# One-core transformer layer (feed-forward, attention, feed-forward): the order of the small steps inside an attention slot, the lag of the first slot, and the entry of the second feed-forward phase

## Chip, cores and metric

One core of a Trainium2 chip. The metric is the time of one execution on the device in microseconds. Lower is better.

## The reference

x has 16 sequences of 256 tokens of 128 channels. The layer is a gated feed-forward block, an attention block, and the same feed-forward block again, each on a layer norm of x and added to x:

```python
x = x + 0.5 * ffn(layernorm(x))      # silu(x W1 s1) * (x W2 s2), two hidden layers of 512 with exact gelu, then W3
x = x + attn(layernorm(x))           # 16 heads of 8 channels: softmax(q k^T / sqrt(8)) v, then Wo + bo
x = x + 0.5 * ffn(layernorm(x))
```

All of it is fp32. The kernel keeps that accuracy with pairs of high and low parts (`act_hi`/`act_lo`, `x_hi`/`x_lo`) for PE's fp32r matmuls.

## The kernel before

The whole x lies in SBUF. There are three phases: `ffn_phase(0)`, attention, `ffn_phase(1)`. Each engine has its own hand-written program, ordered against the others by semaphores only, so the order in which the code calls things is the order in which the engine does them.

**Attention.** A batch is one sequence (256 tokens), 16 batches in 8 pairs. The function `attend(b, ...)` of every engine does one *slot*: slot b computes, in 16 steps u = 0 to 15,

- the row maxima of batch b + 1: PE `max_scores` (L1179, two matmuls a step into one of three rotating banks), DVE `max_unit` (L883, one reduce a step). PE may write a bank again only when DVE has reduced what stood in it, three steps earlier;
- the scores of batch b for the softmax: PE `scores` (L1191 and L1193, four matmuls), ACT `exp_unit` (L678, one exp of 128x512 a step). They run SKEW = 4 steps behind, so units 12 to 15 fall into steps 0 to 3 of the next slot (`in_step`);
- PE `weigh` (L1204): after every fourth unit of scores, sixteen matmuls of probabilities with V, 1.0 us in all. It falls at steps 3, 7, 11 and 15;
- small steps that all use PSUM bank 6 in turn: `max_rows` (u = 1) with ACT `top_max` and DVE `split_max`, which makes `m_parts` for the scores; `transpose_o` and `project_out` of batch b - 2 (u = 3, 5) with ACT `o_to_sbuf` between them and DVE `add_att` (L912, u = 6) behind; `tokens_of_o` of batch b - 1 (L1222), which needs `evacuate_o` (ACT, u = 7), and behind it DVE `norm_o` (L900) and `scale_o` (L904);
- for a pair of batches that comes later, still on bank 6: in odd slots (argument `ahead`) `transpose_att` at u = 7 (L1156), `project_q` at u = 9 (L1161), `project_k` at u = 11 (L1165); in even slots (argument `v_pair`) `project_v` at u = 9 (L1169). ACT copies each out of bank 6 (L571 for q and k). DVE has the layer norm of that pair spread over its steps (`norm_steps`, `normalise`, dictionaries `odd` and `even`).

A **pair of steps** below means an even step and the odd one behind it: their matmuls go to different rows of the array and run together.

q and k then go to DRAM and back, to be laid out by head: ACT `high_part`, POOL `low_part` (L471), SyncE `write_qk` (eight DMAs of 256 KB, L353), and, when all eight have landed, two `load_qk` of 1 MB (L361), the first of which slot 2i + 3 needs at its first step for q and k made in slot 2i + 1. `tokens_of_o` comes at TOKENS = 13, so `norm_o` and `scale_o` come at 14 and 15, and `max_rows` of the next slot waits for `scale_o` (semaphore `o_norm`).

**Behind the last slot.** `attend(NBATCH, own=False)` does the eight steps that are left of batch 15: the last scores, then `transpose_o` and `project_out` of batch 14, and the last weighing at u = 7. `layer1` of the second phase follows: eight tiles, each a gate and an up matmul group (L1092), ACT's silu (L544) and high part (L536), DVE's product (L842) and low part (L833). Between its tiles sit the last small steps for batch 15. ACT loads the gelu table (L518) when the last high part is done (`body`, `first`).

The lines that must be seen exactly:

```python
if u == TOKENS and own and prev:
    if ahead is not None:
        pe.wait_ge(k_full, ahead)
    elif v_pair is not None:
        pe.wait_ge(v_set, v_pair + 1)
    elif prev2:
        pe.wait_ge(att_added, b - 1)
    tokens_of_o(b - 1)
```

Of the kernel before, what the change touches and what calls it, by code (L numbers as in the profile page):

```python
# [27 lines left out]
ACT = mybir.ActivationFunctionType  # L28
# [23 lines left out]
TOKENS = 13  # L52
# [14 lines left out]
def macaron_kernel(nc, x, w_ffn, w_att, s12, sg, s3, bqk, bv, bo, eye, sel, low_rows, out):  # L67
# [11 lines left out]
    with ctx:  # L79
# [210 lines left out]
        def in_step(u, prev, own=True):  # L290
# [105 lines left out]
        def _(pool):  # L396
# [62 lines left out]
            def max_again(b, bb):  # L459

                for qt in range(2):
                    pool.wait_ge(max_done, UNITS * b + 8 * qt + 8)
# [3 lines left out]
                        .then_inc(max_twice, 1)  # L466

# [22 lines left out]
            low_parts(2)  # L490
            pool.wait_ge(bias_set, 1)
            with pool.Fori(1, NPAIR - 2) as i:
                max_again(2 * i, 0)
# [4 lines left out]
                low_parts(i + 2)  # L498
            max_again(NBATCH - 4, 0)
# [13 lines left out]
        def _(act):  # L513
# [24 lines left out]
            def layer1(n0, between={}):  # L538


                for t in range(L1_TILES):
# [55 lines left out]
            def ffn_phase(f):  # L597
                t1, t2, nb = f * NB * HT, f * NP * HID_TILES, f * NB

                def body(i, first=False, more=True):  # L600
# [6 lines left out]
                    if first:  # L607
                        last_product()
                        load_table(ACT.Gelu)
# [55 lines left out]
                else:  # L665
                    layer1(t1, {0: lambda: evacuate_o(NBATCH - 1), 3: lambda: o_to_sbuf(NBATCH - 1)})
# [27 lines left out]
            def attend(b, bb, prev=True, prev2=True, own=True, steps=UNITS, ahead=None, v_pair=None):  # L694


                for u in range(steps):
                    for d, v in in_step(u, prev, own):
                        if v < UNITS:
                            exp_unit(b - d, (bb + d) % 2, v)  # L700
                        if v == UNITS + 3 and own:
                            evacuate_o(b - d)
                    if u == (1 if prev else 0) and own:
                        top_max(b, 6 if prev else 4)
                    if u == 3 and prev2:
                        o_to_sbuf(b - 2)
                    if u == (9 if prev else 5) and v_pair is not None:
# [3 lines left out]
                    if u in (9, 11) and ahead is not None:  # L711
                        full_part(ahead, (u - 9) // 2)
                    if u in (10, 12) and ahead is not None:
                        high_part(ahead, (u - 10) // 2)
# [4 lines left out]
            def att_body(i, par, ahead=True, more=True, first=False):  # L719
                attend(2 * i, 0, prev=not first, prev2=not first, v_pair=(i + 1, 1 - par) if more else None)  # L720
# [779 lines left out]
```

## Time and profile before

| | |
|---|---|
| median of 3 runs | 623.62 us (618.94 to 626.49) |
| the profiled execution, own time | 617.05 us |
| span in its profile | 615.2 us |
| busy: PE, PEld, ACT, DVE, POOL | 589.1, 439.3, 466.4, 443.6, 98.3 us |

The span runs from the first to the last instruction; the profiled execution took 1.9 us more than that. All starts below are in us from the span's start. "PE" is TensorE's matmuls and "PEld" its weight loads, which overlap them; their durations overlap each other too, so the distance from one start to the next says more than a duration. The chain that ended last is followed back from the last instruction, at each step to what released it. A bracket behind an instruction gives the idle time of its engine before it and who ended it. Phase 1 takes about 0 to 204 us, the attention slots 204 to 436, the second feed-forward phase the rest.

### The profile page before, as it was taken

What the parts mean: (1) busy time and instruction counts of PE and PEld (TensorE: products, weight loads), DVE (VectorE), ACT (ScalarE), POOL (GpSimd) and SP (SyncE); (2) the same over time, 40 slices, a digit from 0 to 9 for tenths busy, and PEclk for the clock granted to TensorE, in tenths of its full rate; (3) what the DMA queues carried; (4) which work ended last, traced back from release to release, by engine and by line L of the source; (5) the groups of instructions that cost most, each with busy time, mean ns of one, the idle gap of its engine ahead of it and who ended that gap; (6) DMA issues with size and microseconds to landing.
All of it is one profiled execution on the core that took longest, in us unless ns stands there. A gap on an engine that the chain in (4) does not pass through costs nothing.

```text
span 615.2 us, 12580 instructions
## 1 busy us (share of the span) xinstructions
PE 589.1 (96%) x4452; PEld 439.3 (71%) x4452; DVE 443.6 (72%) x1000; ACT 466.4 (76%) x796; POOL 98.3 (16%) x262
## 2 busy tenths in 40 slices
PE   2999999999999999999999999999989999999996
PEld 2788788788686766565656565766678878788785
DVE  7995855868558778798988897885665756855742
ACT  4677977968865578788787878877877977968964
POOL 2092020022021103132231302102020020020000
PEclk9999999999999799999999999999999999999999
DMA  8300000000074306171625343400000001000011
GB/s 282 86 2 1 0 2 1 0 0 1 1 273 145 130 2 220 56 255 62 235 89 187 137 139 142 134 2 1 2 1 1 1 1 36 0 26 8 1 34 37
DMA packets 36693, 42.02 MB, mean 68 GB/s; under 512 B 2464, under 2 KB 27296, under 8 KB 36640
## 3 DMA queue, kind: packets, MB, share of 16 engines
q1 hardware_dynamic: 36640, 41.31, 19.8%
q8 instruction: 34, 0.56, 0.4%
q14 instruction: 19, 0.16, 0.1%
HBM read 22.42 MB, written 18.87 MB: 67 GB/s over the span
## 4 chain that ended last, share of the span: by engine, by line
PE 73%; ACT 9%; DVE 8%; issue 5%; DMA 3%; SPq 1%; POOL 0%; ACTq 0%; DVEq 0%; POOLq 0%
PE bank L1092 39%; PE bank L1204 9%; PE bank L1179 8%; PE bank L1191 4%; PE bank L1193 3%; DVE silu L842 3%; DVE act_lo L833 2%; ACT silu L544 2%; DVE neg_max L883 2%; PE bank L1161 1%; PE bank L1222 1%; PE bank L1169 1%; ACT act_hi L536 1%; ACT act_hi L559 1%; DMA QK<-qk_scratch 1%
## 5 line engine op out<-in xcount | busy, mean ns | idle before, releaser
L1092 PE MATMUL bank<-act_hi,WH 128*128 128x512 f32 x576 | 230.5, 400 | 3.8 <-ACT act_hi L559 1.5
L1092 PE MATMUL bank<-act_lo,WH 128*128 128x512 f32 x576 | 225.7, 392 | 0.0
L883 DVE TENSOR_REDUCE neg_max<-bank 128x2 f32<-128x512 f32 x256 | 166.8, 681 | 32.6 <-PE bank L1179 30.4
L678 ACT ACTIVATE probs<-bank 128x512 f32<-128x512 f32 x256 | 139.3, 598 | 38.6 <-PE bank L1193 37.0
L853 DVE TENSOR_TENSOR act_lo<-full,act_hi 128x512 fp32r<-128x512 f32 x128 | 91.5, 719 | 101.7 <-ACT act_hi L559 101.4
L557 ACT ACTIVATE full<-bank,SG 128x512 f32<-128x512 f32 x128 | 88.1, 688 | 65.8 <-PE bank L1092 65.0
L1092 PEld LDWEIGHTS bank<-act_hi,WH 128*128 128x128 f32 x576 | 108.2, 188 | 31.2 <-ACT act_hi L559 4.7
L1092 PEld LDWEIGHTS bank<-act_lo,WH 128*128 128x128 f32 x576 | 108.3, 188 | 23.1 <-issue 1.0
L1191 PE MATMUL bank<-QK 32*128 32x256 f32 x512 | 96.1, 334 | 0.4 <-ACT probs L678 0.4
L559 ACT ACTIVATE act_hi<-bank,SG 128x512 fp32r<-128x512 f32 x128 | 87.1, 681 | 0.0
L1193 PE MATMUL bank<-m_parts,SEL 32*128 32x256 f32 x512 | 82.1, 280 | 0.0
L1179 PE MATMUL bank<-QK 32*128 32x256 f32 x512 | 73.4, 334 | 1.8 <-DVE neg_max L883 1.1
L1179 PEld LDWEIGHTS bank<-QK 32*128 32x128 f32 x512 | 46.5, 188 | 38.7 <-issue 18.9
L1204 PE MATMUL bank<-probs,V 128*32 128x256 f32 x1024 | 69.4, 389 | 0.0
L1191 PEld LDWEIGHTS bank<-QK 32*128 32x128 f32 x512 | 64.1, 187 | 2.9 <-ACT probs L678 2.1
L1193 PEld LDWEIGHTS bank<-m_parts,SEL 32*128 32x128 f32 x512 | 64.7, 189 | 0.0
L842 DVE SCALAR_TENSOR_TENSOR silu<-bank,S,silu 128x512 f32<-128x512 f32 x64 | 47.1, 744 | 11.0 <-ACT silu L544 10.0
L1092 PE MATMUL bank<-x_hi,WH 128*128 128x512 f32 x128 | 51.4, 401 | 1.5 <-DVE x_lo L827 1.5
L1092 PE MATMUL bank<-x_lo,WH 128*128 128x512 f32 x128 | 50.6, 395 | 0.0
L544 ACT ACTIVATE silu<-bank,S 128x512 f32<-128x512 f32 x64 | 43.1, 683 | 9.7 <-PE bank L1092 9.6
L833 DVE TENSOR_TENSOR act_lo<-silu,act_hi 128x512 fp32r<-128x512 f32 x64 | 43.9, 686 | 0.7 <-ACT act_hi L536 0.4
L536 ACT ACTIVATE act_hi<-silu 128x512 fp32r<-128x512 f32 x64 | 40.2, 628 | 4.8 <-DVE silu L842 4.7
(94 smaller groups left out, 570.7 us busy)
## 6 DMA issues: line engine op xcount, KB each, us to landing
qk_scratch<-qk SPq DMA_DIRECT2D x64, 256.0 KB, 2.6
QK<-qk_scratch SPq DMA_DIRECT2D x16, 1024.0 KB, 7.6
raw_rest<-w_ffn SPq DMA_DIRECT2D x4, 512.0 KB, 5.8
out<-X SPq DMA_DIRECT2D x4, 512.0 KB, 3.2
X<-x SPq DMA_DIRECT2D x3, 512.0 KB, 7.7
raw<-w_ffn SPq DMA_DIRECT2D x3, 256.0 KB, 4.5
X<-x SPq DMA_DIRECT2D x2, 256.0 KB, 3.2
WA<-w_att SPq DMA_DIRECT2D x1, 256.0 KB, 5.6
```

Of the source, the lines that this page charges most:

```text
L557: A.activation(full[:, t, :], bank[4 + t % 2][:, :], ACT.Gelu, scale=SG[:, layer, t:t + 1])
L559: A.activation(act_hi[1 + layer][:, j, t, :], bank[4 + t % 2][:, :], ACT.Gelu, scale=SG[:, layer, t:t + 1]).then_inc(g_hi, 1)
L678: A.activation(probs[:, v % 8, :], bank[B_BANKS[bb][v]][:, :], ACT.Exp, scale=SCALE)\
L833: D.tensor_tensor(act_lo[0][:, t // HT, t % HT, :], silu[:, t % SLOTS, :], act_hi[0][:, t // HT, t % HT, :].bitcast(F32), op=ALU.subtract)\
L842: D.scalar_tensor_tensor(out=silu[:, t % SLOTS, :], in0=bank[UP_BANKS[t]][:, :], scalar=S12[:, 1, t % HT:t % HT + 1], in1=silu[:, t % SLOT ...
L853: D.tensor_tensor(act_lo[1 + layer][:, j, t, :], full[:, t, :], act_hi[1 + layer][:, j, t, :].bitcast(F32), op=ALU.subtract)\
L883: D.tensor_reduce(neg_max[:, bb, qt, n0:n0 + 2], bank[(banks or A_BANKS[bb])[u]][:, :].rearrange("p (h k) -> p h k", h=2), axis=AX.X, op=A ...
L1092: ins = MM(dst, a, b, start=k == 0, stop=k == len(todo) - 1)
L1179: ins = MM(bank[banks[u]][:, SEQ * i:SEQ * i + SEQ], q_of(2 * par + bb)[rows, 2 * jj + i, P * qt:P * qt + P], k_of(2 * par + bb)[rows, 2 * ...
L1191: MM(dst, k_of(2 * par + bb)[rows, 2 * jj + i, P * kt:P * kt + P], q_of(2 * par + bb)[rows, 2 * jj + i, :], start=True, stop=False)
L1193: ins = MM(dst, SEL[rows, 2 * jj + i, :], m_parts[rows, bb, :], start=False, stop=True)
L1204: ins = MM(bank[4][32 * h:32 * h + 32, SEQ * (g // 2):SEQ * (g // 2) + SEQ], V[par][:, VROW * (2 * bb + kt) + col:VROW * (2 * bb + kt) + c ...
```

## The change

`TOKENS` goes from 13 to 9. In odd slots the order on bank 6 becomes `transpose_att` (u = 7), `tokens_of_o` (9), `project_q` (11), `project_k` (13); in even slots `tokens_of_o` (9), `project_v` (13). The projections now wait for `o_norm` (that is, for `scale_o`), and the tokens for the copy of the transposed x. DVE's norm steps move to free steps. POOL's low parts of q and k move in between the parts of `max_again`. In slot 0 the scores run without lag (steps 0 to 15, weighings at 7, 11, 15), and its `project_v` goes to step 0 of slot 1, on bank 3. In front of the last weighing two tiles of the second `layer1` are computed; `tokens` of batch 15 then come right behind the weighing. The gelu table is loaded directly behind the last silu. In slot 15 and behind it DVE takes over two copies of ACT (`o_to_sbuf`, `evacuate_o`).

```diff
-TOKENS = 13
+TOKENS = 9
...
-            at = [(0, u - SKEW)] if own else []
+            at = [(0, u - SKEW if prev else u)] if own else []
             if prev:
-                at.append((1, u - SKEW + UNITS))
+                at.append((1, u + UNITS if second else u - SKEW + UNITS))
...
+                    if t == L1_TILES - 1 and table is not None:
+                        load_table(table)
                     if t >= 1:
                         product_hi(n0, t - 1)
...
-                            for t, u in enumerate((8, 9, 10, 11))}
+                            for t, u in enumerate((8, 9, 12, 13))}
...
-                    odd = dict(zip((4, 5, 7, 8, 9, 11), norm_steps(norm_of(q), 4 * q, 4, halves=True)))
+                    odd = dict(zip((4, 7, 8, 9, 12, 13), norm_steps(norm_of(q), 4 * q, 4, halves=True)))
...
+                    if u == 4 and not own:
+
+                        pe.wait_ge(exp_done, UNITS * NBATCH - 1 + CREDIT)
+                        layer1(NB * HT, NB, general, tiles=range(2))
...
-                    if u == (9 if prev else 5) and v_pair is not None:
-
-                        if prev2:
-                            pe.wait_ge(att_added, b - 1)
-                        pe.wait_ge(m_lo, b + 1)
+                    if u == 0 and v_pair is not None and second:
+
+                        pe.wait_ge(exp_done, UNITS - 2 + CREDIT)
+                        project_v(v_pair, 3)
+                    if u == 13 and v_pair is not None and not second:
+
+                        pe.wait_ge(o_norm, b)
                         project_v(v_pair, 6)
...
-                    if u == 9 and ahead is not None:
-                        project_q(ahead, 6)
-                    if u == 11 and ahead is not None:
-                        pe.wait_ge(q_full, ahead)
-                        project_k(ahead, 6)
                     if u == TOKENS and own and prev:
 
                         if ahead is not None:
-                            pe.wait_ge(k_full, ahead)
-                        elif v_pair is not None:
-                            pe.wait_ge(v_set, v_pair + 1)
+                            pe.wait_ge(a_xT_sb, ahead + 1)
                         elif prev2:
                             pe.wait_ge(att_added, b - 1)
                         tokens_of_o(b - 1)
+                    if u == 11 and ahead is not None:
+                        pe.wait_ge(o_norm, b)
+                        project_q(ahead, 6)
+                    if u == 13 and ahead is not None:
+                        pe.wait_ge(q_full, ahead)
+                        project_k(ahead, 6)
```

DVE in an odd slot of the steady part, from the moments of the norm (BN_AGGR) on; `neg_max` rows are the reduces of the steps, `o_sum` is `norm_o`, `o_nat` is `scale_o`. Before:

```order
L883 TENSOR_REDUCE neg_max<-bank 128x2
L783 TENSOR_SCALAR var_m<-moments 128x4
L784 TENSOR_SCALAR var<-moments 128x4
L883 TENSOR_REDUCE neg_max<-bank 128x2
L788 TENSOR_SCALAR half<-var 128x4
L883 TENSOR_REDUCE neg_max<-bank 128x2 x2
L793 TENSOR_SCALAR rstd<-half 128x4
L883 TENSOR_REDUCE neg_max<-bank 128x2 x3
L900 RECIPROCAL o_sum<-bank 128x32
L883 TENSOR_REDUCE neg_max<-bank 128x2
L904 TENSOR_TENSOR o_nat<-bank,o_sum 128x256
```

The same place of DVE after:

```order
L893 TENSOR_REDUCE neg_max<-bank 128x2
L793 TENSOR_SCALAR var_m<-moments 128x4
L794 TENSOR_SCALAR var<-moments 128x4
L893 TENSOR_REDUCE neg_max<-bank 128x2
L910 RECIPROCAL o_sum<-bank 128x32
L893 TENSOR_REDUCE neg_max<-bank 128x2
L914 TENSOR_TENSOR o_nat<-bank,o_sum 128x256
L893 TENSOR_REDUCE neg_max<-bank 128x2
L798 TENSOR_SCALAR half<-var 128x4
```

`o_sum` and `o_nat` stand four reduces earlier, directly behind the denser part of the norm; the two last norm steps stand behind them.

PE at the second weighing of such a slot (u = 11). Before, k is projected behind it:

```order
L1204 MATMUL bank<-probs,V 32x256 x8
L1165 MATMUL bank<-xT,WA 128x512
L1179 MATMUL bank<-QK 128x256 x2
L1191 MATMUL bank<-QK 128x256
L1193 MATMUL bank<-m_parts,SEL 128x256
```

After, it is q (L1186), which waits for `o_norm`:

```order
L1229 MATMUL bank<-probs,V 32x256 x8
L1186 MATMUL bank<-xT,WA 128x512
L1204 MATMUL bank<-QK 128x256 x2
L1216 MATMUL bank<-QK 128x256
L1218 MATMUL bank<-m_parts,SEL 128x256
```

Everything of PE behind q in the program, the reduces' matmuls among it, waits when q waits.

## Rows read from the trace of the kernel before

**Rows 1.** The page's busy time of each engine and its share of the span.

```profile
PE 589.1 (96%) x4452; PEld 439.3 (71%) x4452; DVE 443.6 (72%) x1000; ACT 466.4 (76%) x796; POOL 98.3 (16%) x262
```

**Rows 2.** Windows around the first slot: length; busy us of PE, PEld, DVE, ACT, POOL; clock; DMA.

```profile
203.80:207.20 3.40, 2.25 (x20) 1.68 (x18) 3.09 (x7) 0.17 (x1) 1.11 (x2) 1.00 0.59 198
207.20:217.40 10.20, 10.20 (x83) 8.22 (x82) 5.72 (x10) 5.01 (x9) 0.22 (x1) 0.50 0.01 2
```

**Rows 3.** Chain that ended last, slots 8 and 9: start us, us, what.

```profile
319.84 1.00 PE bank L1204 x16
...
333.20 1.00 PE bank L1204 x16
...
342.60 1.12 PE bank L1161 x2
344.42 1.00 PE bank L1204 x16
...
346.52 0.70 ACT qk_full L571
348.64 1.00 PE bank L1204 x16
```

**Rows 4.** Timeline of DVE, slot 9: start us, us, instruction, xcount [idle before].

```profile
338.21 0.69 DVE L883 TENSOR_REDUCE neg_max<-bank 128x2 f32<-128x512 f32 x1 [0.72 <-PE bank L1179]
338.82 0.48 DVE L798 BATCH_NORM_STATS2 stats<-X 128x6 f32<-128x128 f32 x2
339.21 0.67 DVE L883 TENSOR_REDUCE neg_max<-bank 128x2 f32<-128x512 f32 x1
...
340.79 0.41 DVE L912 TENSOR_TENSOR X<-bank,X 128x256 f32<-128x256 f32 x1
341.12 0.68 DVE L883 TENSOR_REDUCE neg_max<-bank 128x2 f32<-128x512 f32 x1
...
341.82 0.28 DVE L778 BATCH_NORM_AGGREGATE moments<-stats 128x2 f32<-128x6 f32 x3
```

**Rows 5.** Timeline of DVE, end of slot 8.

```profile
333.38 0.35 DVE L900 RECIPROCAL o_sum<-bank 128x32 f32<-128x32 f32 x1
333.65 0.63 DVE L883 TENSOR_REDUCE neg_max<-bank 128x2 f32<-128x512 f32 x1
334.19 0.41 DVE L904 TENSOR_TENSOR o_nat<-bank,o_sum 128x256 f32<-128x256 f32 x1
```

**Rows 6.** Timeline of PE, slot 9.

```profile
341.25 0.66 PE L1156 MATMUL bank<-EYE,xn 128*128 128x128 f32 x4 [0.34 <-DVE X L912]
...
347.26 0.66 PE L1222 MATMUL bank<-EYE,oT 128*128 128x128 f32 x4
```

**Rows 7.** SyncE's queue; time from issue to landing of the QK loads; one load in the chain.

```profile
231.65 5.24 SPq L353 DMA_DIRECT2D qk_scratch<-qk  x8
240.41 1.26 SPq L361 DMA_DIRECT2D QK<-qk_scratch  x2
260.56 5.24 SPq L353 DMA_DIRECT2D qk_scratch<-qk  x8
269.68 1.25 SPq L361 DMA_DIRECT2D QK<-qk_scratch  x2
...
318.11 5.33 SPq L353 DMA_DIRECT2D qk_scratch<-qk  x8
325.74 1.26 SPq L361 DMA_DIRECT2D QK<-qk_scratch  x2
...
DMA to landing us min/median/max: 5.9/7.6/9.7
...
240.41 7.40 DMA QK<-qk_scratch
```

**Rows 8.** ACT and PE where the second phase changes from silu to gelu.

```profile
448.97 1.28 ACT L518 ACT_TABLE_LOAD   x1
...
451.67 0.50 PE L1092 MATMUL bank<-act_hi,WH 128*128 128x512 f32 x1 [1.52 <-ACT act_hi L559]
```

More of the change, by code:

```diff
@@ L457, in add_bias, with max_again @@
                     .then_inc(bias_added, 1)
-            def max_again(b, bb):
+            def max_again(b, bb, q=None):
                 for qt in range(2):
+                    if q is not None and qt == 1:
+                        low_part(q, 0)
                     pool.wait_ge(max_done, UNITS * b + 8 * qt + 8)
@@ L710, in attend @@
                         x_to_sbuf(ahead)
[L711 to L714, printed above, removed]
+                    if u in (11, 13) and ahead is not None:
+                        full_part(ahead, (u - 11) // 2)
+                    if u in (12, 14) and ahead is not None:
+                        high_part(ahead, (u - 12) // 2)
                     if u in (1, 2) and not own:
@@ L719, in att_body @@
             def att_body(i, par, ahead=True, more=True, first=False):
-                attend(2 * i, 0, prev=not first, prev2=not first, v_pair=(i + 1, 1 - par) if more else None)
-                attend(2 * i + 1, 1, prev2=not first, ahead=i + 2 if ahead else None)
+                attend(2 * i, 0, prev=not first, prev2=not first,
+                       v_pair=(i + 1, 1 - par) if more and not first else None)
+                attend(2 * i + 1, 1, prev2=not first, more=more, ahead=i + 2 if ahead else None,
+                       v_pair=(1, 1, 3) if first else None)
             att_body(0, 0, first=True)
@@ L1037, in attend @@
                         max_unit(b + 1, 1 - bb, u)
-                    if u == (2 if prev else 0):
-                        split_max(b, bb, 6 if prev else 4)
+                    if u == 2 and prev:
+                        split_max(b, bb)
+                    if u == 3 and not more:
+                        o_to_sbuf(b - 2)
                     if u == 6 and prev2:
                         add_att(b - 2, 2 * b - 4)
+                    if u == 7 and not more:
+                        evacuate_o(b - 1)
                     if u in side:
@@ L1096, in w_of, with layer1 @@
                 return WH[:, c, P * t:P * t + P], WL[:, c, P * t:P * t + P]
-            def layer1(n0, nblk, general, between={}):
-                for t in range(L1_TILES):
+            def layer1(n0, nblk, general, between={}, tiles=range(L1_TILES)):
+                for t in tiles:
                     j, n = t // HT, n0 + t
@@ L1324, in ffn_bodies @@
                     pe.wait_ge(xlo_done, NB + 2)
[L1325 removed]
+                    tokens()
+                    layer1(t1, nb, general, {3: lambda: transpose_o(b), 4: lambda: project_out(b)}, range(2, L1_TILES))
                     pe.wait_ge(att_added, NBATCH)
@@ L1354, in rows_of_max @@
                         pe.wait_ge(o_norm, b - 1)
-                    elif prev:
-                        pe.wait_ge(v_set, pair + 2)
+                    if pair + 1 < NPAIR:
+                        if bb == 0:
+                            pe.wait_ge(k_full, pair + 1)
+                        elif prev2:
+                            pe.wait_ge(v_set, pair + 2)
                     max_rows(b, bb)
+                second = prev and not prev2
                 for u in range(steps):
```

71 lines of the change are left out of this document (43 added, 28 removed).

## Prediction

> **What bounds the kernel now.** I read the page's busy times first, then the granted clock in windows, then the chain that ended last, and in two slots of it the timelines of DVE, PE and SyncE. PE is busy 96% of the span [rows 1], and in the chain the odd slot 9 lasts from 333.20 + 1.00 = 334.20, the end of a weighing, to 348.64 + 1.00 = 349.64, so 15.4 us, and the even slot 8 from 320.84 to 334.20, so 13.4 [rows 3]. But PE does not run freely there. A pair of steps takes 0.70 between q (342.60 + 1.12) and the weighing at 344.42 [rows 3], while DVE needs two reduces for it at 0.61 each (338.21 to 338.82) [rows 4]. A slot has sixteen reduces, 9.7 us, and in an odd slot some 3.4 us of small steps. What the reader is to see is how DVE fares in the first half of slot 9: it works from 338.21 almost without a break until past 342, and PE waits 0.34 us for `add_att` in front of the transposes [rows 4, 6]. PE also waits for ACT's copy of k, done at 347.22, before the tokens at 347.26; a pair of steps covers most of that, 0.14 is left [rows 3, 6]. All removable waits of an odd slot together are about a microsecond. Behind slots 1 to 11 runs a second chain, the way of q and k through DRAM. From the first write to the issue of the load pass 8.8, 9.1 and 7.6 us (231.65 to 240.41, 260.56 to 269.68, 318.11 to 325.74), and a load lands 5.9 us later at the soonest, 7.40 in the one case where it stands in the chain: slot 3 begins when it has landed, 240.41 + 7.40 = 247.81 [rows 7].
>
> **Odd slots with q and k (TOKENS = 9).** The same reduces and small steps in another order; nothing is removed. DVE first, in slot 9's times. Reduce 4 starts at 338.21. Up to the second part of the statistics come four reduces, two statistics of 0.39 and `add_att` 0.33 (340.79 to 341.12) [rows 4]: 2.41 + 0.78 + 0.33 = 3.5, so 341.7. `add_att` now stands ahead of the second statistics and is done 0.39 sooner, which removes PE's 0.34. So PE has the transposes at 340.9 to 341.5, and reduce 8 finds its matmuls at 342.0 (DVE starts about half a microsecond behind the pair's start). Then DVE has reduces 8 to 11 (three of 0.61, the one behind the reciprocal 0.54: 333.65 to 334.19 [rows 5]), moments 0.4 (341.73 to 342.10 [rows 4]), two small steps 0.15, `norm_o` 0.27 and `scale_o` 0.41 [rows 5]: 2.37 + 0.4 + 0.15 + 0.27 + 0.41 = 3.6, so `o_norm` comes at 345.6. PE meanwhile: 341.5, pair 0.70, 0.07 for the copy of x, tokens 0.58, pair 0.80 (0.1 more, since exp and reduces have less cover), weighing 1.00: 344.6. It stands before q for 1.0 us, with every matmul of the slot queued behind. Then q 1.1, pair 0.7, 0.1 for ACT's copy of q (0.70, the row of k's copy [rows 3]), k 1.05, pair 0.7, weighing 1.0: 350.3 against 349.64. The price is +0.7 a slot. Bounds: -0.35, if `scale_o` is done in time and only `add_att`'s wait goes, and +1.2, if DVE falls behind further. I take the worked value; with the slots 3, 5, 7, 9 and 11 it is +3.5.
>
> **Even slots with V.** Tokens and V change places between the same pairs of steps, so PE's cover stays. `norm_o` and `scale_o` stand behind reduces 10 and 11, and two of the four `normalise` steps stand ahead of them. `scale_o` ends about 0.3 us after the pair of steps 12 and 13, and V waits for it. Bounds -0.2 and +0.5; I take +0.2, four slots, +0.8. Slots 12 to 15 carry no q and k and no dense norm; I count them at 0, hidden under reduces and exps as before.
>
> **The way through DRAM.** In slot 7 the writes started at 318.11, 2.7 us before the slot's end at 320.84 [rows 3, 7]. q now starts 3.0 us later (345.6 for 342.60), the end of the slot moves 0.7, so the writes start 0.4 before it. The load lands 7.6 + 5.9 = 13.5 to 9.1 + 5.9 = 15.0 us after that, and the worst case seen is 8.8 + 7.4 = 16.2 [rows 7]. The even slot that covers it lasts 13.6 now. So slot 2i + 3 waits 13.5 - 0.4 - 13.6 < 0, or 1.0, or 2.2. SyncE has only the next load queued behind; on PE the whole slot is. I take 0.5 for each of the five pairs, midway between the two ordinary cases: +2.5. POOL's new order puts k's low part behind the last addition of `max_again`; the writes of q go out first and cover it.
>
> **Slots 0 to 2.** From 203.8 to 207.2 PE is busy 2.25 us of 3.4, and then the granted clock is 0.50, that is 1.2 GHz, for 10.2 us in which PE is busy throughout [rows 2]. With the scores from step 0 on, PE has twelve matmuls for each pair of steps instead of four at that place, so I take it that the clock stays at 2.4 GHz. Slot 0 then has three weighings, 3.0, four pairs behind weighings at 0.7 and four at 1.4 (two reduces and the handing over), 8.4, and 0.9 of waiting at its start: 204.2 to 216.5. V and the missing `project_out` about cancel in slot 1, an odd slot of 15.4 + 0.7, so slot 2 begins near 232.5, where now it is 234.2. But q of the third pair is handed to SyncE 0.4 before, at 232.1 against 231.65 [rows 7], and the load lands 14.9 to 16.2 later, 247.0 to 248.3, where it now lands at 247.81. Almost two microseconds gained are thus taken back by the transfer that nobody saw. I count -0.5 (bounds -1.8 and +0.5).
> The Trainium skill (TensorE: Matmul & The Clock Gate, the table of terms) puts the penalty of a throttled stretch at its time times one minus the clock ratio, here as an estimate 10.2 x 0.5 = 5.1 us. By that the entry would gain 5 us; by the rows, slot 3 cannot begin before its load lands. The page says activity releases the clock, which the fall behind a thin stretch agrees with.
>
> **The end.** The load of the gelu table stands alone in front of the first gelu: 1.28 us from 448.97 on, and PE is idle 1.52 until 451.67 [rows 8]. It moves ahead of two high parts that wait for DVE anyway, where ACT is idle. I take -1.3 (bounds 0 and -1.5). The two tiles in front of the last weighing fill a wait for `project_out`, but the tokens of batch 15, which they covered, now stand uncovered behind the weighing, and the silu of tile 1 stands behind `evacuate_o` as before. The chain from there on is DVE's, and starts with those tokens. I count 0 (bounds -0.6 and +0.6, one tokens step of 0.58).
>
> **Sum.** -0.5 + 3.5 + 0.8 + 2.5 - 1.3 = +5.0. The profiled execution took 617.05 (span 615.2 and 1.9 around it), so 622.1 on its scale. The median of the three runs lies 6.6 above it, and runs without a profile are what is compared, so 628.6.
>
> **Rivals.**
> (B) The clock falls in slots 0 and 1 after all. For: PE and DVE still take turns there, as they did when it fell. Against: PE now has the scores to do in those gaps. At half clock the stretch costs up to 5.1 us more, DVE's 5.72 busy in it [rows 2] hides some; +4.5 on top of the forecast, 633.
> (C) Faster. The mechanism is DVE's arrival at `scale_o`: if reduces queue less than I think and it is done by 344.6, one microsecond sooner than worked out, q never waits, odd slots win 0.35 each, the writes start sooner and the loads land in time. 5 x -0.35 - 1.7 (slot 2 as computed) - 1.3 = -4.8, 618.8, and a little less if V too is free. Against: the sum on DVE leaves no gap to squeeze, and only the reduces' 0.61 could be wrong.
> (D) q waits as said, but the loads land within the longer slots and V does not wait: -0.5 + 3.5 - 1.3 = +1.7, 625.3. For: one of the three write times is only 7.6.
>
> **Chances.** Forecast 0.40, B 0.22, C 0.15, D 0.23. About 1% (6.2 us) is what a measurement of this kernel can tell from no change. Faster by more needs the better half of C: 0.08. Slower by more, over 629.9: nearly all of B and two fifths of the forecast's case, 0.35. Within: 0.57. The range 617 to 636 takes in C's middle and B with the transfer's bounds.
>
> **What would show it.** Right: PE idle of about 1 us before q in odd slots, released by `o_nat` on DVE; odd slots of 16.1 and even ones of 13.6; PE's first reduce matmuls of slots 5 to 13 released by the QK load; clock 1.00 from 204 to 220 and slot 3 still near 247; gelu's start some 1.3 us closer to the last silu. Wrong: q released by nothing but PE itself, which is C; a clock of 0.50 in slot 0 or 1, which is B; slots 5 to 13 without a wait for DMA, which is D.

## The result, and the profile after

The changed kernel took 639.69 us in the median of 6 runs (634.07 to 650.30), the kernel before 621.34 (618.76 to 626.49, 6 runs). The ratio is 1.028, 95% interval 1.0223 to 1.0336: slower by 2.8%, where 628.6 with a range of 617 to 636 had been said. The ratios here leave disturbed runs out; medians and clocks below are over all runs. The profiled execution took 636.72 (span 634.8). Below, "slot 7" and the like are as ahead of the prediction; line numbers are those of the kernel shown.

Page of the changed kernel: span, busy times, and the granted clock in 40 slices.

```profile
span 634.8 us, 12581 instructions
PE 600.1 (95%) x4452; PEld 446.0 (70%) x4452; DVE 444.6 (70%) x1003; ACT 466.1 (73%) x793; POOL 98.6 (16%) x262
PEclk9999999999999659999999999999999999999999
```

PE is busy 11.0 us longer than before [rows 1] with the same number of instructions, so its instructions themselves took longer. The slices say where. The windows of the entry (columns as in [rows 2]) say how much:

```profile
205.90:210.20 4.30, 4.30 (x46) 4.11 (x45) 4.27 (x9) 3.01 (x7) 1.08 (x2) 1.00 0.51 169
210.30:240.90 30.60, 30.60 (x211) 20.82 (x211) 16.70 (x37) 12.90 (x23) 0.67 (x3) 0.50 0.00 1
241.00:254.00 13.00, 12.79 (x164) 7.85 (x166) 10.13 (x20) 10.95 (x22) 6.06 (x17) 1.00 0.46 166
```

The stretch at 0.50 (1.2 GHz) is three times as long as before, 30.7 us against 10.2 [rows 2], and it set in though PE had been busy for all of the 4.3 us ahead of it. Slot 3 begins at 258.7, where it began at 247.81; 2.1 of these 10.9 us passed before the attention began, in parts that the change doesn't touch. PE goes into slot 3 straight from slot 2's last weighing (257.67 + 1.07), so here, unlike before, slot 3's load holds nobody up.

From slot 5's q to slot 7's last weighing, in the chain that ended last:

```profile
300.26 0.34 DVE o_nat L914
...
300.64 1.14 PE bank L1186 x2
...
301.89 0.70 ACT qk_full L575
...
302.63 1.12 PE bank L1190 x2
...
304.45 1.00 PE bank L1229 x16
...
313.75 5.94 DMA QK<-qk_scratch
...
321.96 1.00 PE bank L1229 x16
...
334.88 1.00 PE bank L1229 x16
```

q (L1186) begins when `scale_o` (`o_nat`) ends, and slot 7 when the load lands, 313.75 + 5.94 = 319.69. From weighing to weighing it is 334.88 - 304.45 = 30.4 us; before, 348.64 - 319.84 = 28.8 [rows 3]. The waits by releaser (us in total, times, longest) give both sizes:

```profile
PEld bank L1204 <- DMA QK<-qk_scratch: 7.7, 5, 2.3
PEld bank L1186 <- DVE o_nat L914: 6.9, 6, 1.3
PE bank L1204 <- DMA QK<-qk_scratch: 5.3, 5, 1.8
PE bank L1186 <- DVE o_nat L914: 3.7, 5, 0.9
```

Before, q never waited for `scale_o`, and of the loads only one made a weight load wait, for 0.9 us. The "PE" rows are idle time of the matmuls, the "PEld" rows of the weight loads, which overlap; they don't add up.

At the end, the gelu table is loaded where ACT waits anyway, and PE's idle time before the first gelu matmul fell from 1.52 [rows 8] to 0.15:

```profile
467.33 1.28 ACT L520 ACT_TABLE_LOAD   x1
...
471.08 0.50 PE L1117 MATMUL bank<-act_hi,WH 128*128 128x512 f32 x1 [0.15 <-ACT act_hi L563]
```

The last two weighings, in PE's timeline before and after:

```profile
432.44 1.07 PE L1204 MATMUL bank<-probs,V 128*32 128x256 f32 x16
435.15 1.07 PE L1204 MATMUL bank<-probs,V 128*32 128x256 f32 x16
```

```profile
453.50 1.07 PE L1229 MATMUL bank<-probs,V 128*32 128x256 f32 x16
457.16 1.07 PE L1229 MATMUL bank<-probs,V 128*32 128x256 f32 x16
```

From the end of the last weighing to the end of the span it is 634.8 - 458.23 = 176.6 us, before 615.2 - 436.22 = 179.0, so 2.4 less. But the two tiles now stand between these weighings, which are 3.66 apart instead of 2.71. Over both stretches the end is 1.5 us shorter.

### The profile page after: what moved, and what is told of

It reads as the page before. It is cut to its first block, busy times and chain, and to the rows that moved or that the text cites. A ratio compares the mean times of both kernels' runs of the same rounds, so it can differ in the third digit from the quotient of the medians.

```text
span 634.8 us, 12581 instructions
## 1 busy us (share of the span) xinstructions
PE 600.1 (95%) x4452; PEld 446.0 (70%) x4452; DVE 444.6 (70%) x1003; ACT 466.1 (73%) x793; POOL 98.6 (16%) x262
## 4 chain that ended last, share of the span: by engine, by line
PE 68%; ACT 9%; DVE 8%; DMA 6%; issue 6%; SPq 2%; POOL 0%; ACTq 0%; POOLq 0%; DVEq 0%
PE bank L1117 38%; PE bank L1229 7%; PE bank L1204 7%; DMA QK<-qk_scratch 5%; PE bank L1216 3%; PE bank L1218 3%; DVE neg_max L893 3%; ACT silu L546 2%; DVE silu L852 2%; DVE act_lo L843 2%; ACT act_hi L538 2%; PE bank L1261 1%; PE bank L1186 1%; ACT act_hi L563 1%; PE bank L1190 1%
## 5 line engine op out<-in xcount | busy, mean ns | idle before, releaser
L683 ACT ACTIVATE probs<-bank 128x512 f32<-128x512 f32 x256 | 140.8, 599 | 44.1 <-PE bank L1218 43.0
L1216 PE MATMUL bank<-QK 32*128 32x256 f32 x512 | 98.0, 335 | 0.4 <-ACT probs L683 0.4
L1218 PE MATMUL bank<-m_parts,SEL 32*128 32x256 f32 x512 | 84.8, 284 | 0.0
L1204 PE MATMUL bank<-QK 32*128 32x256 f32 x512 | 77.4, 339 | 5.5 <-DMA QK<-qk_scratch 5.3
L1204 PEld LDWEIGHTS bank<-QK 32*128 32x128 f32 x512 | 49.4, 193 | 44.3 <-issue 18.9
L1229 PE MATMUL bank<-probs,V 128*32 128x256 f32 x1024 | 72.9, 405 | 0.0
L1216 PEld LDWEIGHTS bank<-QK 32*128 32x128 f32 x512 | 66.3, 191 | 2.9 <-ACT probs L683 2.2
L1218 PEld LDWEIGHTS bank<-m_parts,SEL 32*128 32x128 f32 x512 | 67.0, 194 | 0.0
```

Of the source, the lines that this page charges most:

```text
L683: A.activation(probs[:, v % 8, :], bank[B_BANKS[bb][v]][:, :], ACT.Exp, scale=SCALE)\
L1204: ins = MM(bank[banks[u]][:, SEQ * i:SEQ * i + SEQ], q_of(2 * par + bb)[rows, 2 * jj + i, P * qt:P * qt + P], k_of(2 * par + bb)[rows, 2 * ...
L1216: MM(dst, k_of(2 * par + bb)[rows, 2 * jj + i, P * kt:P * kt + P], q_of(2 * par + bb)[rows, 2 * jj + i, :], start=True, stop=False)
L1218: ins = MM(dst, SEL[rows, 2 * jj + i, :], m_parts[rows, bb, :], start=False, stop=True)
L1229: ins = MM(bank[4][32 * h:32 * h + 32, SEQ * (g // 2):SEQ * (g // 2) + SEQ], V[par][:, VROW * (2 * bb + kt) + col:VROW * (2 * bb + kt) + c ...
```

## The experiments

Every run has its mean granted clock (most profiles have the clock at half in the last microseconds of the span too, 3.0 at most, which counts in it). Over the 97 runs of the kernel before beside these experiments it lies between 0.977 and 0.996 (median 0.984), and the time goes with it, from 615 to 625 us. Half-clock time of a run is 2 x (1 - clock) x its time. Among runs of the same kernel, over all kernels, a run was 0.38 us longer per microsecond of it. The column "at 0.99" takes each run to a clock of 0.99 by that slope and gives the mean with about its 95% bounds; it separates what the engines wait for from what the clock takes. It is a fit, and rough where a kernel has no run near 0.99.

| kernel | runs | median us | before, same chip | clock | at 0.99 |
|---|---|---|---|---|---|
| before | 97 | 620.7 | | 0.977 to 0.996 | 618.3 ± 0.2 |
| changed | 6 | 639.7 | 621.3 | 0.955 to 0.975 | 629.4 ± 1.7 |
| `first_only` | 6 | 626.4 | 618.8 | 0.972 to 0.998 | 619.0 ± 0.6 |
| `order_only` | 6 | 632.1 | 618.8 | 0.969 to 0.995 | 629.9 ± 0.7 |
| `end_only` | 12 | 619.4 | 618.8 | 0.976 to 0.997 | 616.9 ± 0.5 |
| `after_lag` | 6 | 636.9 | 618.8 | 0.959 to 0.991 | 630.0 ± 1.6 |
| `even_only` | 12 | 620.8 | 621.3 | 0.980 to 0.993 | 619.8 ± 0.6 |
| `norms_away` | 6 | 639.4 | 621.3 | 0.971 to 0.982 | 632.3 ± 0.7 |
| `tokens_8` | 6 | 640.1 | 620.5 | 0.945 to 0.985 | 631.7 ± 1.5 |
| `half_load` | 6 | 627.1 | 620.3 | 0.980 to 0.991 | 624.0 ± 0.7 |
| `first_lanes` | 12 | 625.8 | 620.3 | 0.972 to 0.991 | 618.7 ± 0.7 |
| `end_fill_1024` | 12 | 623.9 | 620.3 | 0.998 to 1.000 | |
| `end_fill_one` | 12 | 621.9 | 620.5 | 0.978 to 1.000 | 621.8 ± 0.5 |
| `end_fill_two_one` | 12 | 623.0 | 620.5 | 0.979 to 1.000 | 622.4 ± 0.4 |
| `end_fill_all` | 6 | 629.4 | 621.3 | 0.977 to 0.983 | 624.4 ± 0.8 |
| `first_fill` | 6 | 644.9 | 621.3 | 0.959 to 0.967 | 631.0 ± 0.6 |
| `after_fill` | 6 | 668.4 | 620.5 | 0.945 to 0.984 | |
| `after_half` | 7 | 630.5 | 621.3 | 0.972 to 0.979 | 622.7 ± 0.7 |
| `after_lag_half` | 12 | 624.8 | 621.3 | 0.981 to 0.995 | 622.6 ± 0.7 |

### The change in three parts, and all but one

The kernels set the parts by flags; the code cuts below are written out for the value that the run has.

`first_only` is the kernel before with the changed first slot (scores without lag, V of pair 1 at step 0 of slot 1), `order_only` with the new order on bank 6 (with its norm steps and POOL's low parts), `end_only` with the three edits at the end. `after_lag` is the changed kernel without the first-slot part:

```diff
-            at = [(0, u - SKEW if prev else u)] if own else []
+            at = [(0, u - SKEW)] if own else []
             if prev:
-                at.append((1, u + UNITS if second else u - SKEW + UNITS))
+                at.append((1, u - SKEW + UNITS))
...
-                    if u == 0 and v_pair is not None and second:
-                        pe.wait_ge(exp_done, UNITS - 2 + CREDIT)
-                        project_v(v_pair, 3)
+                    if u == 5 and v_pair is not None and not prev:
+                        pe.wait_ge(m_lo, b + 1)
+                        project_v(v_pair, 6)
```

> The kernel before with one part of the change: slot 0 scores without lag, and V of pair 1 is made at step 0 of slot 1. Theory 1 (the first slot of the change is what keeps the clock low three times as long): the granted clock stands at 0.50 from about 3 us after the start of slot 0 for about 31 us instead of 10.24, the mean clock of the execution falls from 0.99 to about 0.975, and the time is 7 to 9 us above the kernel before (about 629). Rival 1 (the long stretch at half clock comes from something else, such as the later start of this execution or a draw of the chip): mean clock 0.99 and 0.5 us less than before (about 621), as the prediction had the entry alone. The QK loads and q are as before in either case.

> The kernel before with the new order on bank 6 alone (tokens at step 9, q and k at 11 and 13, V at 13, DVE's norm steps and POOL's low parts moved); the first slot and the end are as before. Theory 1 (two costs that don't depend on each other: clock at the entry, q and QK load in the steady pairs): mean clock 0.99, five pairs at 30.4 to 31.2 us instead of 28.8, so 9 to 10 us above the kernel before (about 631). Rival 2 (the steady pairs are longer only because the half clock at the entry put the engines out of step): pairs near 28.8 us and at most 2 us above. The prediction's own size of this part: +6.8 us.

> The kernel before with the parts of the change at the end alone: two tiles of the second first layer in front of the last weighing, the gelu table behind the last silu, DVE in place of ACT for two copies. Both theories: clock 0.99 and faster by what the part behind the last weighing lost in the changed kernel, 2.4 us (about 619); the prediction had 1.3 us.

> The changed kernel with the first slot as before (lag of four steps, V of pair 1 at step 5 of slot 0), all else changed. Theory 1: mean clock back at 0.99, 10 to 12 us below the changed kernel, that is about 7 us above the kernel before (9.5 for the five steady pairs, less 2.4 for the end). Rival 1: as the changed kernel, about 18 us above before, clock 0.975.

At an equal clock the parts are +0.7 (first slot), +11.6 (order) and -1.4 (end) against 618.3, in sum +10.9; the changed kernel has +11.1. So apart from the clock the parts add up. The medians add up worse: the ratios were 1.018 (1.0115 to 1.0245) for `order_only`, 1.0159 (1.009 to 1.0228) for `after_lag` and 0.9987 (0.9948 to 1.0025) for `end_only`. Five of six runs of `first_only` had clocks of 0.972 to 0.977, and the sixth 0.998 and 614.52 us, where the kernel before has 615.1 to 617.9 at 0.995 or 0.996. That is the only run of this kernel near full clock, too little to say that the part gains anything there.

Two expectations fell. `end_only`'s profile had 27.3 us at 0.50 in a slot 0 that is the same as before, so one long stretch is no mark of the changed slot. It also gained 1.4 at an equal clock where 2.4 was expected: the 2.4 had left out the 0.95 that the two tiles add in front of the last weighing. And `after_lag` did not come back to a clock of 0.99. Both are taken up below.

### The steady pairs

`order_only`, chain that ended last, slots 7 and 8 and the load for slot 9 (its L1199 and L1203 are q and k, L1242 a weighing); then, from PE's timeline, slot 6's last weighing and the wait in front of slot 7:

```profile
317.35 1.00 PE bank L1242 x16
...
322.54 0.34 DVE o_nat L924
...
322.92 1.14 PE bank L1199 x2
...
324.90 1.13 PE bank L1203 x2
...
326.73 1.00 PE bank L1242 x16
329.90 1.00 PE bank L1242 x16
...
333.45 1.00 PE bank L1242 x16
...
336.29 6.08 DMA QK<-qk_scratch
...
309.55 1.07 PE L1242 MATMUL bank<-probs,V 128*32 128x256 f32 x16
311.57 0.38 PE L1217 MATMUL bank<-QK 32*128 32x256 f32 x1 [0.95 <-DMA QK<-qk_scratch]
```

Read by the distances of the weighings, a pair of slots is 30.86 long here and 28.80 before. The odd slot's steps 7 to 15 take 326.73 - 317.35 = 9.38, before 8.72 (+0.66). The even slot's take 6.90, before 6.64 (+0.26). From its last weighing to the next slot's first it is 4.31, before 3.17 (+1.14). The last difference is the wait for the load; in front of slots 5, 7, 9, 11 and 13 it is 0.99, 1.01, 1.14, 0.90 and 1.60, 1.13 in the mean. The even slots 4, 6, 8 and 10 have +0.26 or +0.27 each, slot 12 has +0.05. Four kernels took these apart.

`even_only`: the new order in even slots alone (tokens at 9, V at 13; odd slots as before).

> The kernel before with the new order in even slots alone (tokens at step 9, V at 13, DVE's four normalise steps at 8, 9, 12, 13); odd slots, first slot and end as before. Theory 1 (the loss in the steady pairs, 1.9 to 2.05 us a pair, is in the odd slots: q waits 0.8 to 0.9 us for scale_o, and the QK load ends 1.0 us late): pairs at 28.8 us and no more than 1 us from the kernel before. Rival (part of it sits in even slots, where V waits for scale_o in the same manner; the prediction had 0.2 us a slot): up to 0.9 us a pair, so 4 us above before.

Ratio 1.0004 (0.9975 to 1.0033); pairs of 29.07, +0.27 each. The odd slots carry nearly all of the loss, and the even slots the +0.26 seen above.

`half_load`: `order_only`, and the QK loads of pairs 2 to 7 bring q alone, so their scores are made with k of an earlier pair.

```diff
-            def load_qk(ring):
+            def load_qk(ring, rows=8):
...
-                sp.dma_start(QK[:, RING - 1 - ring, :, :, :].rearrange("p w j t -> p (w j) t").bitcast(F32),
-                             qk_scratch[par].rearrange("r c w j t -> (r c) (w j) t")[:, :, t0:t0 + SEQ])\
+                sp.dma_start(QK[:, RING - 1 - ring, :, :, :].rearrange("p w j t -> p (w j) t")[:, 0:rows, :].bitcast(F32),
+                             qk_scratch[par].rearrange("r c w j t -> (r c) (w j) t")[:, 0:rows, t0:t0 + SEQ])\
...
-                    load_qk(2 * par + bb)
+                    load_qk(2 * par + bb, 4)
```

> The new order on bank 6 alone, with the QK loads of pairs 2 to 7 cut to their first half (q; k of the pair isn't loaded anew, so the scores are of other data). It had 11 us above before at an equal clock: about 1.14 us a pair where PE waits for the QK load, 0.66 where q waits for scale_o, 0.26 in the even slot. Theory (the load's landing is one of the waits and lies on the path): half of 1 MB lands 1 to 1.4 us earlier, PE's idle time for the load goes from 5.2 us to under 1, pairs of 29.7 to 29.9 us, 5 us less than the new order alone (about 626 to 627). Rival (the load isn't what ends the wait; something else is ready at the same time): pairs still 30.8 us, 631.

Its list of waits has no row for the load any more, that for q is unchanged:

```profile
PEld bank L1204 <- DVE o_nat L929: 7.5, 6, 1.4
PE bank L1204 <- DVE o_nat L929: 4.6, 6, 0.9
```

Pairs are 29.70, so 1.16 less, and 5.9 us are gone at an equal clock: the load's landing was on the path, for its full size. All six runs had clocks of 0.980 to 0.991, where `order_only`'s six spread from 0.969 to 0.995; the means of the clocks are the same, 0.984 and 0.983.

`norms_away` and `tokens_8` go at the wait for q: `order_only` with DVE's norm steps of the odd slots at 0, 1, 12, 13, 14, 15, and `order_only` with the odd slots' tokens a step sooner.

```diff
-                    odd = dict(zip((4, 7, 8, 9, 12, 13), norm_steps(norm_of(q), 4 * q, 4, halves=True)))
+                    odd = dict(zip((0, 1, 12, 13, 14, 15), norm_steps(norm_of(q), 4 * q, 4, halves=True)))
```

> The new order on bank 6 in all slots (as in the run that had it alone: pairs of 30.86 us, 11 us above before at an equal clock), with DVE's norm steps of odd slots at steps 0, 1, 12, 13, 14, 15 in place of 4, 7, 8, 9, 12, 13, so that none stands in front of norm_o and scale_o. Theory 1 (the q wait is DVE's queue, and the QK wait is a wait of its own): the wait of q for o_nat (4.6 us of PE's idle time in all) goes, the QK wait stays near 1.0 us a pair, and the time falls by 4 to 5 us against the new order alone, pairs near 30.0. Rival (DVE is behind by its row maxima anyway, or the QK load simply ends the wait whatever goes before): no gain, pairs still 30.8.

> The new order on bank 6 alone, with the tokens of odd slots at step 8 instead of 9 (norm_o and scale_o at 9 and 10, q still at 11). There PE stands 0.8 us a pair for scale_o, and 0.5 when the norm steps are elsewhere. Theory (norm_o and scale_o at 10 and 11 stand behind the row maxima of their own steps in DVE's queue, and q at 11 needs them with no step to spare): the wait of q goes to 0.2 us or less, w7 to w15 of the odd slot from 9.38 to 8.9, pairs 0.4 to 0.7 us shorter, 2 to 3 us in all; the QK wait stays at 1.0. Rival (the tokens then wait as long for the copy of xT, or DVE is late in any case): no difference beyond 0.2 us a pair.

Both miss. PE's idle time before q fell from 4.6 us to 3.2 and to 2.0, and the kernels didn't get faster: pairs of 31.05 and 30.71, against 30.86 at the same place. With the norm steps away, steps 3 to 7 of the odd slot took 3.93 for 3.55, probably since two of them now stand in front of `split_max`. With the tokens at 8, steps 7 to 11 took 4.09 for 3.78 and 11 to 15 took 5.14 for 5.60. So most of what q no longer waits comes back elsewhere in the slot. The reading of this is that DVE has no step to spare in these slots, and q at 11 needs what DVE puts out at 11; no run with less work on DVE tested it.

### The clock in steady slots

`tokens_8` shows where else the clock falls: windows behind the arrival of a QK load, and the load's row in the chain (it lands at 404.23).

```profile
398.00:404.60 6.60, 4.96 (x76) 3.23 (x74) 4.22 (x8) 3.87 (x7) 0.22 (x1) 1.00 0.71 231
404.70:414.80 10.10, 10.10 (x84) 5.91 (x80) 5.82 (x10) 5.09 (x10) 0.91 (x2) 0.50 0.17 55
```

```profile
398.27 5.96 DMA QK<-qk_scratch
```

The profiled executions of `order_only`, `after_lag` and `norms_away` have such stretches too (6.8 us from 280.7; 3.4 from 345.5 and 3.4 from 407.0; 13.7 from 409.1), each close behind a wait for a load. No profile of a kernel without these waits has one from slot 3 on, other than in the last 3 us of the span. Such stretches would explain why `after_lag` didn't come back to 0.99, and why single runs of these kernels go as low as 0.945; those runs have no profile. In these profiles the fall comes 0.3 to 2.7 us behind the end of a wait of 0.85 to 1.64 us. Nearly every load is waited for, though, and behind most of these waits the clock stays: the changed kernel's own profile has five, the longest 1.82 us, and no fall behind any of them. The half loads' effect on the clock is uneven too. The mean clock rose from 0.967 to 0.974 in the changed kernel and from 0.976 to 0.987 without its first slot (`after_half` and `after_lag_half`, below), but not in `order_only`. So the order of events is shown, a cause only made likely.

### The clock in the first two slots

With the waits for the load gone from the steady slots, the first slot can be judged. `after_half` is the changed kernel with the half loads, `after_lag_half` the same with the lag restored.

> The changed kernel with the QK loads of pairs 2 to 7 cut to their first half (k of these pairs isn't loaded anew). The same cut on the new order alone took the waits for the load away, 5.8 us at an equal clock, and with them the falls of the clock in the steady pairs: all six runs had 0.980 to 0.991. Theory (two places where the clock falls: the entry, long without a lag, and the waits for the QK load): clock 0.972 to 0.977 in most runs, tight, and 629 to 632 us, 8 to 10 below the changed kernel. Rival (the first slot has no part in the clock): clock 0.98 to 0.99, 625.

> The same cut with the first slot's lag restored. Theory: clock 0.980 to 0.991, and 624 to 626 us: 5 to 6 below the one without a lag, all of it clock. Rival: no difference between the two beyond 1 us.

Windows of `after_half` and of `after_lag_half`:

```profile
206.70:230.50 23.80, 23.80 (x170) 16.82 (x170) 12.24 (x21) 9.82 (x18) 0.44 (x2) 0.50 0.01 2
230.60:245.00 14.40, 13.31 (x155) 8.19 (x155) 11.33 (x31) 11.43 (x23) 4.55 (x13) 1.00 0.22 82
```

```profile
210.30:223.80 13.50, 13.50 (x111) 9.79 (x110) 7.47 (x13) 6.51 (x13) 0.44 (x2) 0.50 0.00 1
223.90:245.00 21.10, 20.09 (x259) 12.53 (x260) 17.09 (x41) 16.79 (x34) 5.74 (x17) 1.00 0.28 101
```

The two kernels differ in the first slot alone. Their clocks don't overlap (0.972 to 0.979 and 0.981 to 0.995), their medians are 5.8 us apart, and at an equal clock they are the same. The first slot without a lag costs 5.8 us here, all of it clock.

`first_lanes` tested one reason for it. Without a lag the row-maximum matmuls and the scores of a step go to the same 32 rows and queue up, with a lag they go to different ones. It is `first_only` with

```diff
-                qt, jj, lane = a_unit(u)
+                qt, jj, lane = a_unit(u ^ 4 if b == 1 else u)
```

on PE and DVE.

> The kernel before with the first slot of the change (no lag), and with the units of batch 1's row maxima taken in another order (unit u with bit 2 flipped), so that in one step of slot 0 the row-maximum matmuls and the scores go to different groups of 32 rows, as they do with the lag. In the changed kernel's slot 0 both went to the same group, one matmul behind the other: 0.60 us a step at full clock, and 5.34 us for four steps and a weighing at half clock, where the kernels with a lag took 4.93. Theory A (the same row group is what makes the long stretch at 0.50 and its cost): clock near 0.985, 620 us or less. Theory B (the length of the stretch is not set by that): four steps at half clock in 4.9 us, so 1.2 to 1.6 us less than without the new order, clock still 0.972 to 0.977 in most runs, about 625.

Theory B: 9 of 12 runs at 0.972 to 0.974, median 625.75, ratio 1.0088 (1.0051 to 1.0126). Four steps and a weighing at half clock took 4.9 us (weighings at 209.62 and 214.54) instead of 5.34, and the stretch was as long, 34.1 us (30.7 in `first_only`'s profile).

`end_fill_1024` tested another: that the clock falls because slot 0 has few matmuls over all 128 rows until weighings set in. It has `end_only`'s edits and, for the second batch's row maxima, in a bank that is about to be written,

```diff
                 wait(pe, max_done, UNITS * b + u - used_last(banks, prev, u) + 1)
+                if b == 1:
+                    for n in (512, 512):
+                        MM(bank[banks[u]][:, 0:n], WH[:, 0, 0:P], WH[:, 1, 0:n], start=True, stop=True)
```

> The end of the change and two matmuls of 128 rows by 512 columns in front of the row-maximum matmuls of all sixteen steps of slot 0 (the run before had two of them at steps 0 to 3, where the clock stayed at full, and one of 256 columns at steps 4 to 15, where it fell at 216.9). Theory (what holds the clock is the amount of 128-row work a stretch has): no stretch at 0.50 in slot 0, mean clock 0.995 or more; the added work takes about 0.4 us a step, 6.4 us in all, so about 621 us. Rival (the clock falls whatever PE does there, and two of 512 only happened to coincide with a later fall): clock 0.98, 628 to 632 us.

```profile
206.00:224.00 18.00, 18.00 (x113) 10.97 (x112) 9.52 (x15) 5.46 (x10) 0.81 (x3) 1.00 0.08 27
224.00:240.00 16.00, 15.92 (x170) 9.52 (x170) 11.76 (x30) 11.39 (x21) 0.77 (x2) 1.00 0.01 3
```

All 12 runs had 0.998 or more, and in the profile the clock stayed full in the slots behind, where nothing was added. The price was higher than the gain: a step took 1.33 us, so 623.93 in the median, ratio 1.0074 (1.0045 to 1.0103). Less work cost less and held the clock less often. `end_fill_one`, one matmul of 512 columns at steps 0 to 10, had 0.999 or more in 5 of 12 runs (615.4 to 617.5 us) and 0.978 to 0.994 in the others; ratio 0.9988 (0.9943 to 1.0033). `end_fill_two_one`, two at steps 0 to 3 and one at 4 to 10: 1.0019 (0.9974 to 1.0064). `end_fill_all`, two at steps 0 to 3 and one of 256 columns at 4 to 15: 1.0132 (1.0093 to 1.0172); its profile has the clock at full for steps 0 to 3, and the fall at 216.9. `first_fill`, one of 256 columns at each step of `first_only`'s slot 0: 1.0384 (1.0345 to 1.0423), with 41.0 us at 0.50 in the profile.

> The kernel before with the end of the change, and one matmul of 128 rows by 512 columns at each of steps 0 to 10 of slot 0, where no weighing falls; none at steps 11 to 15. With two at all sixteen steps the clock was 1.00 in all runs and the time 624. Theory: one is enough to hold the clock in most runs (0.995 or more); cost 0.2 us a step, 2.2, against a gain of 5 to 7 us of the clock: about 615. Rival: one of 512 is too little, as one of 256 was: clock 0.98, 621 or more.

> As the last, with two matmuls of 512 columns at steps 0 to 3 (where PE has no scores and waits for DVE) and one at steps 4 to 10. Theory: clock 0.998 or more in all runs; cost 1.6 us for steps 0 to 3 and 1.4 for 4 to 10: about 615 to 616. Rival: clock 0.98 to 0.985 with a fall two or three us behind step 4, 622.

> The kernel before with the parts of the change at the end, and with matmuls of all 128 rows that nobody reads put in front of slot 0's row-maximum matmuls, in the same bank: two of 512 columns at steps 0 to 3, one of 256 at steps 4 to 15. Theory (the clock falls in slot 0 because PE there does only matmuls of 32 rows, one group at a time, with waits between them; without that load it had a median clock of 0.983 to 0.990, with 10.24 to 27.31 us at 0.50 in the traces): the stretch at 0.50 in slot 0 is gone or shorter, the mean clock is 0.995 or more, and the time is about 614, 5 us below before. Rival (the clock falls for another reason, such as the end of phase 1's dense work): stretches as before, and the time is 1 to 3 us longer than without the added matmuls, some 619 to 621.

> The kernel before with the first slot of the change (no lag), and one matmul of 128 rows by 256 columns in front of each step's row-maximum matmuls of slot 0. Without them five of six runs had a clock of 0.972 to 0.977 and took 625.4 to 628.7 us, one had 0.998 and took 614.5. Theory: clock of 0.995 or more in most runs, 614 to 616 us. Rival: clock as without them, about 627 us.

The same cure on the changed kernel failed. `after_fill` puts the two matmuls at all steps of slot 0 and at steps 0 to 10 of slot 1.

> The changed kernel with two matmuls of 128 rows by 512 columns in front of the row-maximum matmuls of all steps of slot 0 and of steps 0 to 10 of slot 1. Without a lag no weighing falls into slot 0's steps 0 to 6, nor into slot 1's steps 4 to 10 (there the next one after step 3 comes at step 11); with a lag the only such stretch is slot 0's steps 0 to 10. Theory (the changed kernel's long stretch at 0.50 is lack of 128-row work in these two stretches, and it costs 8 us or more of the 18): mean clock 0.998 to 1.000 and no stretch at 0.50 before slot 2. The time by parts: the kernel before at full clock about 615, + 10 to 11 for the steady pairs, - 2 for the end, - 1 for the first slot, + 0.4 us for each of 27 steps with added work = 11, so 633 to 634, against 637 to 640 without it. Rival: the clock falls in slot 1 all the same (0.97 to 0.98), 645 or more.

It took 668.43, ratio 1.0666 (1.0573 to 1.0760), with clocks of 0.945 to 0.984, and its profile alternates between full and half clock from 216.0 to 243.3. The clock is not the larger part of that: the profiled run had 0.984, more than any run of the changed kernel, and still took 655.48 us, 18.8 more than the changed kernel's profiled run at 0.975. The added work itself, with the waits that it makes, costs most of it, where 0.4 us a step had been expected. So for the slot without a lag it isn't shown that this kind of work holds the clock, and what makes its stretch longer stays open. What differs for certain is that with a lag slot 1 has weighings at steps 3, 7, 11 and 15, and without one at 3, 11 and 15.

No version here is faster than the kernel before by more than the measurement can tell. The nearest is `end_only`, 1.4 us below it at an equal clock and 0.9987 (0.9948 to 1.0025) in the runs as they came.

## Why the prediction was wrong

The forecast was +5.0 on its own scale and the result is +18.3 in medians. By steps:

- **Odd slots, q behind `scale_o`: right.** Worked out +0.7 a slot with a wait of about 1.0; measured +0.66, with up to 0.9 of idle time on PE and the q row right behind `o_nat`.
- **Even slots: right.** +0.2 said for four slots, +0.26 and +0.27 measured in these four; slot 12 makes a V too and was counted at nothing, +0.05 measured.
- **The way through DRAM: right in kind, half the size.** This is the other term that failed. SyncE's queue has

```profile
305.06 5.81 SPq L353 DMA_DIRECT2D qk_scratch<-qk  x8
313.75 1.25 SPq L361 DMA_DIRECT2D QK<-qk_scratch  x2
```

  so the writes of slot 5 went out 0.4 before the slot's end at 305.45, as said, and the load landed 14.6 us later, at 319.69 (13.5 to 15.0 said). I took 0.5 "midway between the two ordinary cases", which are none and 1.0. "None" stood on the one way of 7.6 us from first write to load. In the changed kernel these ways are 8.7 to 9.2 in all five pairs, so the wait was there each time, 0.90 to 1.60 in `order_only`, 1.13 in the mean: 5.7 in all for 2.5 said.
- **Slots 0 to 2: the step that failed.** The sum has -0.5 for them, on a clock that stays up. "I take it that the clock stays at 2.4 GHz", because PE has more matmuls in the gaps. PE was busy all through them and the clock fell nonetheless. This is rival B's event, with its price: 5.8 us (4.5 said). I gave it 0.22. The evidence used was one stretch in one execution, of something that varies from run to run by 10 us of time: the kernel before itself ranges from 0.977 to 0.996.
- **A cost that no rival had: clock lost behind the new waits.** Taking half of each load away brought 639.7 to 630.5, so 9.2 us, of which five waits are 5.7. The other 3.5 I put down to the clock, with the reservations above; by the column at 0.99 it is 6.7 of waits and 2.5 of clock.
- **The end: right.** -1.3 said; -1.4 at an equal clock, and -1.5 in the profile from the last weighing but one. That it is the table and not the two tiles or the copies rests on PE's idle time before the first gelu matmul; no run took the three edits apart.

The sum by what the runs show: 5 x 0.66 + 4 x 0.26 + 5 x 1.13 - 1.4 + 5.8 + 3.5 = +17.9, against 18.3 measured. So close a match is luck, and the fit says so: at an equal clock the changed kernel is +11.1, where the first four terms give 8.6, and its clock is 18.3 - 11.1 = 7.2, where the last two give 9.3. Of the 2.5 that are missing at an equal clock about one is slot 1's wait for q: from its second weighing to its last `order_only` takes 9.26 us, the kernel before 8.28. The rest stays open. Either way loads and clock together are 13 to 15 us of the 18.3; the forecast had 2.5 for the loads and nothing for the clock.

The conditions of rivals C and D can be read in the profile after: PE's weight loads waited for `scale_o` in front of q in all six odd slots that make a q, which rules out C, and for the loads of slots 5 to 13 all five times, which rules out D.

The rule of the Trainium skill that the prediction weighed (TensorE: Matmul & The Clock Gate, the table of terms: a throttled stretch costs its time times one minus the clock ratio, half of it here) gives more than these runs paid. Over all kernels the cost was 0.38 us per microsecond at half clock, and 0.32 over the 97 runs of the kernel before, presumably because DVE, which keeps its pace, hides a part.

## What to carry to other kernels

A transfer that just fits behind other work should be counted at its full lateness in every round of a steady loop, not at the mean of "late" and "in time": here all five rounds took the late case, 0.9 to 1.6 us each. When an order is changed in a loop of this kind, the slack between a value and its use on an in-order engine (q at step 11, `scale_o` at step 11) is the first thing to count, in steps. And before a single profile's clock is read as a property of the kernel, the clocks of its runs are worth a look: here they alone move the time by 10 us.

## What the runs showed of the hardware

- The clock can be at half for very different times at the same steps: in slot 0 with a lag, which is the same code in all these kernels, 3.4, 10.2, 13.7, 17.1, 20.5, 23.9 and 27.3 us were seen in profiles.
- It fell in stretches in which the profile has PE busy throughout (4.3 of 4.3 us in the changed kernel), and stayed at half for 20 us and more with PE busy all the time. A busy PE in the profile doesn't tell its clock. The Trainium skill (TensorE: Matmul & The Clock Gate, the HAM clock gate) has a busy array get its full clock back; here it stayed at half for 30.6 us of a PE that was busy throughout, so the measurement decides.
- With two matmuls of 128 rows by 512 columns in each of slot 0's steps the clock was 0.998 or more in 12 of 12 runs, and in the profile at full there and through all later slots, where the kernel before had at best 0.996; in a slot 0 without lag the same matmuls did not hold it.
- The clock also falls in steady slots, behind waits of about one microsecond, in some executions of a kernel and not in others.
